# Image pooling on 96 partitions, two channel products instead of six, sink values in PSUM, and the order of two queues

## The chip, the cores and the metric

The kernel runs on one core of one Trainium2 chip. The metric is the device time of one execution in microseconds. Three executions of the kernel before took 2934.99, 2945.84 and 2946.96 us, so the median is 2945.84 us. Engines go by the names of the profile: PE is TensorE's matmul, PEld its weight load, DVE VectorE, ACT ScalarE, POOL GpSimd, SP SyncE, whose queue only issues DMAs.

## What is computed

For 64 batches, an image of 12 channels by 224 by 224 is summed over patches of 16 by 16 and its channels are mixed into 192 features. That gives 14 x 14 = 196 tokens, to which 32 text tokens are appended. Then come a layer norm, causal attention with 12 heads, rotary angles and a sink value per head, a residual, a second norm and a mixture of 8 experts with two choices per token.

```
pooled = x.reshape(B, C, n, 16, n, 16).sum(axis=(3, 5))          # n = 14
h = einsum('bcij,ce->bije', pooled, channel_weights)             # 196 x 192 per batch
h = concat([h, txt], axis=1)                                     # 228 tokens
att = softmax(concat([sink_h, mask(q k^T / 4)]))[..., 1:]        # per head
h = h + (att v W_proj + b_proj) * rezero
h = h + moe(layernorm(h))                                        # top 2 of 8, capacity 4560
```

## The kernel before, in words

There are two passes. Pass 1 takes the batches, pass 2 the experts' rows in 160 tiles. The change touches pass 1 and the setup ahead of it.

Pass 1 is a software pipeline. In step i, batch i is pooled (`p`), batch i-1 is normed, projected to q, k and v, and rotated (`a`), batch i-2 has the maxima of its scores taken (`m`), batch i-3 gets its softmax and attention (`t`), and batch i-4 its output projection, residual, second norm and routing (`z`). Each engine runs a list written out by hand in one order per step: `step_tensor`, `step_scalar`, `step_vector`, `pass1_gpsimd` and `pass1_sync`. Engines meet at semaphores only, and each runs strictly in its own order, so a waiting instruction holds up all that stands behind it.

The image lies on 112 partitions: 3 groups (g) of 4 channels by 28 half patch rows, each partition with 8 image rows of 224 columns. `load_image` (L404) is one DMA of contiguous runs of 8 x 224 numbers, 7168 bytes. On POOL, `fold_image` (L682) adds the lower 4 rows to the upper 4, one instruction of 896 elements a partition for each g. On DVE, `pool_image` (L497) sums what is left to 14 patch columns. On POOL, `spread_patches` (L689) multiplies by the 0/1 table `patch`, which puts each half row's sum into the column of its own patch row; three instructions. On PE, `sum_channels` (L837) then needs 2 x 3 products, for two halves of the tokens and three groups, which also sum the partitions.

The order around it, in each step:

- PE: the scores and `score_t` products, `attend` 0 to 2, `T0 T1 T2` (`turn_qk`, L894), `turn_shift` (L934), `make_v`, `turn_y`, `T3 T4 T5`, `sum_channels`, `turn_yn` (L998), and from the next step on `S0 C0`, `project` and so on.
- DVE: `norm1_stats`, `max_scores` 0, `residual`, `norm2_stats`, maxima 1 and 2, `pool_image` 0, `rotate` 0, maximum 3, `pool_image` 1, `rotate` 1, maxima 4 and 5, `choose`, maximum 6, `pool_image` 2, maxima 7 and 8, `make_shift` (L573), `assign` (L659), `place_k` 1, `split_shift` (L583), `weigh` (L638), `place_k` 3, `normalize` 0 and 1 (L589), `place_k` 5.
- ACT, late in the step: `place_q` 0, `copy_y`, `round_shift`, `place_q` 2, `copy_v`, `place_q` 4, `copy_h`, `copy_yn`.
- POOL: `inverse_std` of norm 1, fold 0, `inverse_std` of norm 2, fold 1, `add_rotation` 0, fold 2, `add_rotation` 1, `low_parts` 0 and 1 (L722), `spread_patches`, and four indirect DMAs of `scatter_rows`.
- SP: `load_image` of the batch after `p`, `store_h2`, `load_text` of `p`, and in the first 20 steps `fill_slots`, which writes 1453.5 KB of filler rows to HBM.

Waits that matter here: `turn_shift` waits for `shift_made` and for `routed`, which `assign` raises with its fifth instruction (L675). `turn_yn` waits for `y_normed` of `normalize` 1. `split_shift` waits for `shift_rounded` of ACT. `T0` waits for `qk_low` of both `low_parts`. `choose` uses and `weigh` writes small operands in columns 32 to 63 of PSUM bank 7.

Of the kernel before, what the change touches and what calls it, by code (L numbers as in the profile page):

```python
# [21 lines left out]
GRP = 4  # L22
NG = CH // GRP
XP = GRP * SIDE * 2
XF = HALF * IMG
D = 192
# [22 lines left out]
def constants(tokens):  # L49
# [29 lines left out]
    rows = np.arange(XP)  # L79
# [10 lines left out]
        "patch": ((rows[:, None] // 2) % SIDE == np.arange(SIDE)[None]).astype(f),  # L90
# [5 lines left out]
               "before", "patch", "filler"]  # L96
# [28 lines left out]
def build(nc, x, txt, chan_w, norm_scale, norm_bias, w_attn, b_attn, w_proj, b_proj, sinks,  # L125
# [17 lines left out]
    with ctx:  # L143
# [23 lines left out]
        patch = sb("patch", [XP, SIDE])  # L167
        filler = sb("filler", [TT, 2, 2, RW], u32)
        chan = sb("chan", [XP, NG, D])
# [5 lines left out]
        sink_tok = sb("sink_tok", [TT, HEADS])  # L175
        sink_key = sb("sink_key", [128, HEADS])
# [5 lines left out]

        arena = sb("arena", [128, 2 * NG * XF])
        xin = [arena[0:XP, NG * XF * i:NG * XF * (i + 1)].rearrange("p (g f) -> p g f", g=NG) for i in range(2)]
        pooled = [sb(f"pooled{i}", [XP, NG, SIDE]) for i in range(2)]
        spread = sb("spread", [XP, NG, SIDE * SIDE])
# [68 lines left out]
        def view(parts, a, b):  # L255
            nonlocal taken
            taken += a * b
            assert taken <= 2 * NG * XF
            return arena[0:parts, taken - a * b:taken].rearrange("p (a b) -> p a b", a=a)
# [41 lines left out]
        x_spread = sem("x_spread")  # L301
# [52 lines left out]
        N_SMALL = 25  # L354


        def setup_sync(sp):
            for dst, src in (
                (cos[:, :, :], const["cos"]), (sin[:, :, :], const["sin"]), (ident[:, :], const["ident"]),
                (split[:, :], const["split"]), (small[:, :], const["small"]),  # L360
                (patch[:, :], const["patch"]), (filler[:, :, :, :], const["filler"]),
# [38 lines left out]
        x_img = x.rearrange("b (g c) (q r) w -> b (c q) g (r w)", g=NG, r=HALF)  # L400
# [23 lines left out]
        def setup_vector(dve):  # L424
# [28 lines left out]
            nc.vector.tensor_scalar(sink_tok[:, :], sink_tok[:, :], 4.0, None, ALU.mult)  # L453
# [43 lines left out]
        def pool_image(dve, at, g):  # L497

            if g == 0:
                wait(dve, x_spread, at.b - 1)  # L500
# [1202 lines left out]
```

## Time and profile before

| | |
|---|---|
| three executions | 2934.99, 2945.84, 2946.96 us |
| the profiled execution: time | 2942.38 us |
| its span, first to last instruction | 2940.6 us |
| busy share PE, DVE, POOL, ACT | 95%, 70%, 69%, 58% |
| mean granted TensorE clock | 0.983 of full speed |
| pass 1, from the first channel product to the last `turn_shift` | 42.0 to 1724.8 us |

A row of the timeline is the start in us, the duration in us, the engine, the line, the operation, output<-input, the shapes and xcount, which is the number of instructions merged into the row; in brackets stands the idle time before it and what ended it. The end of a PE row is modelled and overlaps the next row, so intervals on PE are read from start to start. A PE product on plain fp32 data appears as two records. A DMA row of a window gives the packets, the MB and the share of sixteen DMA engines' time that the queue's packets took.

### The profile page before, as it was taken

The page shows a single profiled execution, that of the slowest core. Times are in us where ns is not written, and L with a number is a line of the kernel's source. Part 1 is how long each engine was busy: PE and PEld are TensorE (multiplying, and loading weights), DVE is VectorE, ACT ScalarE, POOL GpSimd, SP SyncE. Part 2 cuts the span into 40 slices and gives each one's busy share as a digit, 9 for nine tenths or more (in the row PEclk, how much of TensorE's full clock was granted, in tenths as well). Part 3 has the DMA queues.
Part 4 walks back from the last instruction along what each step waited for, and adds up shares of the span by engine and source line. Part 5 has one row for each costly group of instructions (what it writes and reads, how often), then busy time and mean ns, then how long its engine had stood idle before and what let it go on. Part 6 is the DMA issues. An engine that isn't in the chain of part 4 may idle for free. (4 is left out here: it accounts for less than half of the span.)

```text
span 2940.6 us, 65980 instructions
## 1 busy us (share of the span) xinstructions
PE 2788.6 (95%) x21712; PEld 2515.0 (86%) x21712; DVE 2049.6 (70%) x5657; ACT 1692.5 (58%) x4074; POOL 2022.5 (69%) x2070
## 2 busy tenths in 40 slices
PE   2899999999999999999999976999999999999998
PEld 1788888888888888888888866999999989999997
DVE  3577777777777777777777745767676767676766
ACT  1466666666665666666566644655565656565655
POOL 3578888888888888788888733655566555565655
PEclk9899999999999999999999988999999999999999
DMA  6455455544443444444344222333333333323242
GB/s 191 141 176 175 167 165 173 156 122 122 115 107 106 119 121 122 119 111 111 107 121 121 56 48 61 56 60 51 63 55 65 49 65 49 65 45 65 46 68 43
DMA packets 206006, 292.47 MB, mean 99 GB/s; under 512 B 95670, under 2 KB 167675, under 8 KB 205874
## 3 DMA queue, kind: packets, MB, share of 16 engines
q1 hardware_dynamic: 82642, 241.41, 28.2%
q0 software_dynamic: 122880, 47.00, 11.4%
q10 hardware_dynamic: 352, 2.41, 0.3%
q8 instruction: 69, 1.13, 0.2%
q14 instruction: 63, 0.52, 0.1%
HBM read 201.73 MB, written 93.90 MB: 101 GB/s over the span
## 5 line engine op out<-in xcount | busy, mean ns | idle before, releaser
L1493 POOL DMA_INDIRECT out<-arena,who x320 | 595.3, 1860 | 291.4 <-DVE who L1372 180.5
L571 DVE TENSOR_REDUCE top<-bank 114x2 f32<-114x456 f32 (+1 forms) x576 | 352.8, 622 | 87.3 <-PE bank L930 71.1
L686 POOL TENSOR_TENSOR arena<-arena 112x896 f32<-112x896 f32 x192 | 403.0, 2100 | 13.2 <-DMA arena<-in_x 13.2
L1466 PE MATMUL bank<-w_dn,hid 128*114 128x192 f32 x3840 | 401.9, 264 | 0.0
L1466 PEld LDWEIGHTS bank<-w_dn,hid 128*114 128x114 f32 x3840 | 390.3, 180 | 0.0
L1439 ACT ACTIVATE arena<-bank 128x456 f32<-128x456 f32 x320 | 176.3, 551 | 342.1 <-PE bank L1430 332.2
L1284 POOL DMA_INDIRECT moe_rows<-row,slot x256 | 294.4, 1150 | 103.9 <-issue 85.0
L548 ACT ACTIVATE pieces<-bank 64x456 fp32r<-64x456 f32 x384 | 209.4, 545 | 147.1 <-PE bank L906 144.9
L1443 DVE TENSOR_TENSOR arena<-bank,arena 128x456 f32<-128x456 f32 x320 | 201.5, 630 | 96.6 <-ACT arena L1439 84.6
L726 POOL TENSOR_TENSOR qk<-rot_c,qk 114x384 fp32r<-114x384 f32 x256 | 253.8, 1013 | 19.0 <-ACT qk L747 19.0
L1426 PE MATMUL bank<-pieces 128*128 128x456 f32 x640 | 241.2, 377 | 21.9 <-DVE arena L1443 15.2
L805 ACT ACTIVATE prob<-bank 115x456 f32<-115x456 f32 x384 | 208.0, 542 | 78.0 <-PE bank L956 77.3
L1430 PE MATMUL bank<-pieces 128*128 128x456 f32 x640 | 238.5, 373 | 0.0
L1455 DVE TENSOR_TENSOR hid<-arena,hid 128x456 fp32r<-128x456 f32 x320 | 201.6, 630 | 52.3 <-ACT hid L1450 34.3
L1429 PE MATMUL bank<-pieces 128*128 128x456 f32 x640 | 237.9, 372 | 0.0
L1450 ACT ACTIVATE hid<-arena 128x456 fp32r<-128x456 f32 x320 | 186.9, 584 | 88.1 <-DVE arena L1443 86.7
L1428 PE MATMUL bank<-pieces 128*128 128x456 f32 x640 | 237.5, 371 | 0.0
L1427 PE MATMUL bank<-pieces 128*128 128x456 f32 x640 | 236.8, 370 | 0.0
L1483 POOL TENSOR_TENSOR rms<-rms,minus_half 114x4 f32<-114x4 f32 x82 | 85.4, 1042 | 193.5 <-DVE rms L1364 193.5
L906 PE MATMUL bank<-ident_r,qk 114*128 114x114 f32 x1536 | 202.1, 282 | 10.7 <-POOL qk L726 10.7
L502 DVE TENSOR_REDUCE pooled<-arena 112x14 f32<-112x896 f32 x192 | 206.5, 1076 | 6.4 <-POOL arena L686 6.4
L906 PEld LDWEIGHTS bank<-ident_r,qk 114*128 114x128 f32 x1536 | 186.5, 196 | 23.0 <-POOL qk L726 23.0
(171 smaller groups left out, 7216.3 us busy)
## 6 DMA issues: line engine op xcount, KB each, us to landing
arena<-in_x SPq DMA_DIRECT2D x63, 2352.0 KB, 11.8
arena<-moe_rows SPq DMA_DIRECT2D x82, 363.4 KB
moe_rows<-filler SPq DMA_DIRECT2D x20, 1453.5 KB
out<-h SPq DMA_DIRECT2D x64, 171.0 KB
out<-arena,who POOLq DMA_INDIRECT x320, 5.0
arena<-in_w_t SPq DMA_DIRECT2D x9, 512.0 KB
arena<-in_w_t SPq DMA_DIRECT2D x18, 256.0 KB
moe_rows<-row,slot POOLq DMA_INDIRECT x256, 7.3
```

The costliest lines, as they stand in the source:

```text
L571: nc.vector.tensor_reduce(dst, src, AX.X, ALU.max).then_inc(maxed[k], 1)
L686: nc.gpsimd.tensor_tensor(xin[at.par][:, g, 0:mid], xin[at.par][:, g, 0:mid], xin[at.par][:, g, mid:XF], ALU.add).then_inc(x_folded, 1)
L726: ins = nc.gpsimd.tensor_tensor(lo, of, first.bitcast(fp32), ALU.subtract)
L906: ins = nc.tensor.matmul(dst[:, TT * (2 * pair + half):TT * (2 * pair + half + 1)], src, ident_r[0:TT, 0:TT], start=True, stop=True)
L1284: nc.gpsimd.indirect_dma_start(out=moe_rows[0:SLOTS, :], out_offset=bass.IndirectOffsetOnAxis(ap=slot[at.par][:, 2 * t + k:2 * t + k + 1], ...
L1426: nc.tensor.matmul(dst, hi[:, 0, col], za_hi[:, :], start=True, stop=False)
L1427: nc.tensor.matmul(dst, hi[:, 0, col], za_lo[:, :], start=False, stop=False)
L1428: nc.tensor.matmul(dst, lo[:, 0, col], za_hi[:, :], start=False, stop=False)
L1429: nc.tensor.matmul(dst, hi[:, 1, col], zb[:, :], start=False, stop=False)
L1430: ins = nc.tensor.matmul(dst, lo[:, 1, col], zb[:, :], start=False, stop=True)
L1466: ins = nc.tensor.matmul(dst, hid2[:, j, h_part, at], w_dn2[e_par][:, j, w_part, :], start=(j == 0 and s % 2 == 0 and part == 0), stop=(j ...
L1493: nc.gpsimd.indirect_dma_start(out=out[:, :], out_offset=bass.IndirectOffsetOnAxis(ap=who[par][:, s:s + 1], axis=0), in_=ys[par][:, s, :], ...
```

## The change

- The image lies on 96 partitions instead of 112: partition 12 r + c holds channel c, the two image rows 2r and 2r+1 of each of the 14 patch rows. `load_image` is 8 DMAs, one for each r, each to 12 partitions in runs of 1792 bytes (`x_loaded` counts 8 x 16).
- `fold_image` and `pool_image` work in bands of patch rows, 5, 5 and 4 of 14. A fold has 1120, 1120 and 896 elements a partition; `pool_image` reduces over 16 neighbouring columns alone.
- `spread_patches`, the table `patch` and the semaphore `x_spread` are gone. `sum_channels` has 2 products with 96 rows to sum over; `chan` holds each channel's weights 8 times over and is loaded by one DMA.
- `sink_tok` times 4 is written to columns 480 to 491 of PSUM bank 7, and `make_shift` reads it there.
- DVE: `assign` moves from behind `make_shift` to ahead of maxima 7 and 8, where `pool_image` 2 was; `pool_image` 2 moves behind `place_k` 1, ahead of `split_shift`.
- POOL: fold 2 moves from between the two `add_rotation` to behind `low_parts` 1, where `spread_patches` was.

```diff
-GRP = 4
-NG = CH // GRP
-XP = GRP * SIDE * 2
-XF = HALF * IMG
+XP = CH * HALF
+XF = 2 * IMG
+BANDS = ((0, 5), (5, 10), (10, SIDE))
+NG = len(BANDS)
...
+        sink_top = bank[7][0:TT, 480:480 + HEADS]
...
-            for g in range(NG):
-                sp.dma_start(chan[:, g, :], chan_w[GRP * g:GRP * (g + 1), :].unsqueeze(1)
-                             .to_broadcast([GRP, SIDE * 2, D])).then_inc(loaded, 16)
+            sp.dma_start(chan[:, :], chan_w.unsqueeze(0).to_broadcast([HALF, CH, D])).then_inc(loaded, 16)
...
-        x_img = x.rearrange("b (g c) (q r) w -> b (c q) g (r w)", g=NG, r=HALF)
+        x_img = x.rearrange("b c (i r s) w -> b r c i (s w)", r=HALF, s=2)
...
             wait(sp, x_pooled, NG * (at.b - 1))
-            sp.dma_start(xin[at.par][:, :, :], x_img[at.b, :, :, :]).then_inc(x_loaded[at.par], 16)
+            for r in range(HALF):
+                sp.dma_start(xin[at.par][CH * r:CH * (r + 1), :, :], x_img[at.b, r, :, :, :]).then_inc(x_loaded[at.par], 16)
...
-            nc.vector.tensor_scalar(sink_tok[:, :], sink_tok[:, :], 4.0, None, ALU.mult)
+            nc.vector.tensor_scalar(sink_top, sink_tok[:, :], 4.0, None, ALU.mult)
...
             ins = nc.vector.tensor_reduce(
-                pooled[at.par][:, g, :],
-                xin[at.par][:, g, 0:XF // 2].rearrange("p (r j c) -> p j r c", r=HALF // 2, c=PATCH), AX.XY, ALU.add)
+                pooled[at.par][:, SIDE * lo:SIDE * hi],
+                xin[at.par][:, lo:hi, 0:IMG].rearrange("p i (j c) -> p i j c", c=PATCH), AX.X, ALU.add)
...
-                                    sink_tok[:, :].unsqueeze(1).unsqueeze(1).to_broadcast([TT, 2, 2, HEADS]),
+                                    sink_top.unsqueeze(1).unsqueeze(1).to_broadcast([TT, 2, 2, HEADS]),
...
-            mid = XF // 2
-            nc.gpsimd.tensor_tensor(xin[at.par][:, g, 0:mid], xin[at.par][:, g, 0:mid], xin[at.par][:, g, mid:XF],
+            lo, hi = BANDS[g]
+            nc.gpsimd.tensor_tensor(xin[at.par][:, lo:hi, 0:IMG], xin[at.par][:, lo:hi, 0:IMG], xin[at.par][:, lo:hi, IMG:XF],
                                     ALU.add).then_inc(x_folded, 1)
...
-            pe.wait_ge(x_spread, n)
+            pe.wait_ge(x_pooled, NG * n)
             wait(pe, v_ready, at.b)
             for t, (lo, hi) in enumerate(((0, TT), (TT, SIDE * SIDE))):
-                for g in range(NG):
-                    ins = nc.tensor.matmul(bank[6][0:hi - lo, D * t:D * (t + 1)], spread[:, g, lo:hi], chan[:, g, :],
-                                           start=(g == 0), stop=(g == NG - 1))
+                ins = nc.tensor.matmul(bank[6][0:hi - lo, D * t:D * (t + 1)], pooled[at.par][:, lo:hi], chan[:, :],
+                                       start=True, stop=True)
...
             maxima("6")
-            if p:
-                pool_image(dve, p, 2)
+            if z:
+                assign(dve, z)
             maxima("7 8")
             if m:
                 make_shift(dve, m)
-            if z:
-                assign(dve, z)
             if a:
                 place_k(dve, a, 1)
+            if p:
+                pool_image(dve, p, 2)
             if m:
                 split_shift(dve, m)
...
                 if a:
                     add_rotation(pool, a, 0)
-                if p:
-                    fold_image(pool, p, 2)
-                if a:
                     add_rotation(pool, a, 1)
                     low_parts(pool, a, 0)
                     low_parts(pool, a, 1)
                 if p:
-                    spread_patches(pool, p)
+                    fold_image(pool, p, 2)
```

## Rows read from the trace of the kernel before

**Rows 1.** The page's part 1: busy us, share of the span, instructions.

```profile
PE 2788.6 (95%) x21712; PEld 2515.0 (86%) x21712; DVE 2049.6 (70%) x5657; ACT 1692.5 (58%) x4074; POOL 2022.5 (69%) x2070
```

**Rows 2.** Busy time of a stretch of pass 1 by engine, clock, DMA share, GB/s.

```profile
700.00:1200.00 500.00, 494.62 (x4240) 436.86 (x4243) 372.02 (x1127) 304.99 (x678) 404.63 (x504) 1.00 0.43 117
```

**Rows 3.** Timeline of PE, from one step's T0 into the next step.

```profile
1005.77 1.55 PE L906 MATMUL bank<-ident_r,qk 114*128 114x114 f32 x12
...
1010.74 2.16 PE L844 MATMUL bank<-chan,spread 112*114 112x192 f32 x12
1012.74 0.56 PE L1003 MATMUL bank<-ident,yn 114*97 114x114 f32 x4
...
1031.33 1.55 PE L906 MATMUL bank<-ident_r,qk 114*128 114x114 f32 x12
1033.21 0.39 PE L939 MATMUL bank<-ident,shift 114*128 114x114 f32 x2 [0.33 <-DVE slot L675]
```

**Rows 4.** PE timeline: the channel products of two steps, 57 steps apart.

```profile
211.91 2.16 PE L844 MATMUL bank<-chan,spread 112*114 112x192 f32 x12
...
1680.88 2.16 PE L844 MATMUL bank<-chan,spread 112*114 112x192 f32 x12
```

**Rows 5.** Idle time of PE before L939, 195:1740: ended by, us, times.

```profile
  DVE slot L675: 12.5, 35
```

**Rows 6.** Timeline of DVE at make_shift in the same two steps.

```profile
1005.98 0.21 DVE L578 TENSOR_TENSOR shift<-top,sink_tok 114x48 f32<-114x48 f32 x1
...
1031.51 0.60 DVE L578 TENSOR_TENSOR shift<-top,sink_tok 114x48 f32<-114x48 f32 x1
```

**Rows 7.** Timeline of POOL: low_parts 1, spreads, a fold, spreads of the next step.

```profile
1003.58 1.99 POOL L726 TENSOR_TENSOR qk<-rot_c,qk 114x384 fp32r<-114x384 f32 x2 [0.27 <-ACT qk L747]
1005.52 1.53 POOL L694 TENSOR_TENSOR spread<-pooled,patch 112x196 f32<-112x196 f32 x3
...
1023.66 2.11 POOL L686 TENSOR_TENSOR arena<-arena 112x896 f32<-112x896 f32 x1
...
1031.05 1.48 POOL L694 TENSOR_TENSOR spread<-pooled,patch 112x196 f32<-112x196 f32 x3
```

**Rows 8.** PE timeline of the first step that has no image.

```profile
1701.44 1.55 PE L906 MATMUL bank<-ident_r,qk 114*128 114x114 f32 x12
...
1707.79 0.63 PE L1003 MATMUL bank<-ident,yn 114*97 114x114 f32 x4 [1.30 <-DVE yn L598]
```

**Rows 9.** DVE timeline of that step, from split_shift on.

```profile
1704.34 0.45 DVE L586 SCALAR_TENSOR_TENSOR shift_t<-shift_hi,split,bank 128x228 fp32r<-128x228 f32 x1 [1.01 <-ACT shift_hi L795]
...
1707.31 0.42 DVE L598 TENSOR_TENSOR yn<-bank,rden 114x96 f32<-114x96 f32 x2
```

**Rows 10.** Instructions of L502 (pool_image): durations ns min/median/max.

```profile
L502 DVE TENSOR_REDUCE pooled<-arena x69: 1073/1077/1078, 709.1 to 1287.7; 112x14 f32<-112x896 f32 x69
```

**Rows 11.** Hardware queue in 305.5:309.5 (fillers), 1006:1016 (one image), 1752:1760 (weights), 300:500.

```profile
q1 hardware_dynamic: 321, 0.52, 37.3%
...
q1 hardware_dynamic: 352, 2.41, 88.0%
...
q1 hardware_dynamic: 1069, 1.44, 84.2%
...
q1 hardware_dynamic: 12159, 32.08, 47.4%
```

**Rows 12.** Windows of a filler step: DMA share and GB/s are the last two columns.

```profile
306.00:309.00 3.00, 3.00 (x38) 2.59 (x37) 2.40 (x12) 2.18 (x6) 2.27 (x3) 1.00 0.38 135
...
305.00:306.00 1.00, 1.00 (x10) 0.92 (x9) 0.35 (x1) 0.04 (x1) 1.00 (x3) 1.00 0.24 69
325.00:326.00 1.00, 1.00 (x7) 0.60 (x4) 0.02 (x1) 0.73 (x2) 1.00 (x2) 1.00 0.15 48
```

**Rows 13.** Start of the run: first channel products on PE, first norm statistics on DVE.

```profile
42.00 4.16 PE L844 MATMUL bank<-chan,spread 112*114 112x192 f32 x12 [7.65 <-DMA w_qkv<-rot_s]
...
50.36 0.62 DVE L515 BATCH_NORM_STATS2 st<-h 114x6 f32<-114x192 f32 x2 [10.87 <-DMA h<-in_txt]
```

More of the change, by code:

```diff
@@ L78, in constants @@
             filler[:, par, s, COL_ID] = tokens + (par * T + 2 * q + s) % ROWS
-    rows = np.arange(XP)
     return {
@@ L89, in constants @@
         "before": (q[:, None] < q[None, :]).astype(f),
-        "patch": ((rows[:, None] // 2) % SIDE == np.arange(SIDE)[None]).astype(f),
         "filler": filler,
@@ L95 @@
 CONST_NAMES = ["cos", "sin", "ident", "mask_q0", "mask_k", "sel", "split", "small",
-               "before", "patch", "filler"]
+               "before", "filler"]
 class Batch:
@@ L166, in build @@
         ones = sb("ones", [TT, TT], bf16)
-        patch = sb("patch", [XP, SIDE])
         filler = sb("filler", [TT, 2, 2, RW], u32)
-        chan = sb("chan", [XP, NG, D])
+        chan = sb("chan", [XP, D])
         scale_col = sb("scale_col", [C, 2])
@@ L179, in build @@
         gate = sb("gate", [C, 2, E])
[L183 to L186, printed above, removed]
+        arena = sb("arena", [128, 2 * SIDE * XF])
+        xin = [arena[0:XP, SIDE * XF * i:SIDE * XF * (i + 1)].rearrange("p (i f) -> p i f", i=SIDE) for i in range(2)]
+        pooled = [sb(f"pooled{i}", [XP, SIDE * SIDE]) for i in range(2)]
         h = [sb(f"h{i}", [TT, 2, D]) for i in range(2)]
@@ L257, in view @@
             taken += a * b
-            assert taken <= 2 * NG * XF
+            assert taken <= 2 * SIDE * XF
             return arena[0:parts, taken - a * b:taken].rearrange("p (a b) -> p a b", a=a)
@@ L300, in build @@
         x_pooled = sem("x_pooled")
-        x_spread = sem("x_spread")
         h_summed = sem("h_summed")
@@ L352, in build @@
         added = [sem(f"added{i}") for i in range(2)]
-        N_SMALL = 25
+        N_SMALL = 22
         def setup_sync(sp):
@@ L360, in setup_sync @@
                 (split[:, :], const["split"]), (small[:, :], const["small"]),
-                (patch[:, :], const["patch"]), (filler[:, :, :, :], const["filler"]),
+                (filler[:, :, :, :], const["filler"]),
                 (scale_col[:, :], norm_scale.rearrange("(c p) -> p c", p=C)),
@@ L499, in pool_image @@
             if g == 0:
-                wait(dve, x_spread, at.b - 1)
+                wait(dve, h_summed, at.b - 1)
             dve.wait_ge(x_folded, NG * at.b + g + 1)
+            lo, hi = BANDS[g]
             ins = nc.vector.tensor_reduce(
-                pooled[at.par][:, g, :],
-                xin[at.par][:, g, 0:XF // 2].rearrange("p (r j c) -> p j r c", r=HALF // 2, c=PATCH), AX.XY, ALU.add)
+                pooled[at.par][:, SIDE * lo:SIDE * hi],
+                xin[at.par][:, lo:hi, 0:IMG].rearrange("p i (j c) -> p i j c", c=PATCH), AX.X, ALU.add)
             ins.then_inc(x_pooled, 1)
@@ L682, in fold_image @@
         def fold_image(pool, at, g):
-            pool.wait_ge(x_loaded[at.par], 16 * (at.half + 1))
-            mid = XF // 2
-            nc.gpsimd.tensor_tensor(xin[at.par][:, g, 0:mid], xin[at.par][:, g, 0:mid], xin[at.par][:, g, mid:XF],
+            pool.wait_ge(x_loaded[at.par], 16 * HALF * (at.half + 1))
+            lo, hi = BANDS[g]
+            nc.gpsimd.tensor_tensor(xin[at.par][:, lo:hi, 0:IMG], xin[at.par][:, lo:hi, 0:IMG], xin[at.par][:, lo:hi, IMG:XF],
                                     ALU.add).then_inc(x_folded, 1)
-        def spread_patches(pool, at):
-            wait(pool, h_summed, at.b)
-            for g in range(NG):
-                pool.wait_ge(x_pooled, NG * at.b + g + 1)
-                ins = nc.gpsimd.tensor_tensor(spread[:, g, :].rearrange("p (i j) -> p i j", j=SIDE),
-                                              pooled[at.par][:, g, :].unsqueeze(1).to_broadcast([XP, SIDE, SIDE]),
-                                              patch[:, :].unsqueeze(2).to_broadcast([XP, SIDE, SIDE]), ALU.mult)
-            ins.then_inc(x_spread, 1)
         def inverse_std(pool, at, norm):
```

1 line of the change is left out of this document (removed).

## The prediction

> **What bounds the kernel now.** I read the page's busy shares first, then the busy time of a stretch of pass 1, then the timelines of PE, DVE and POOL in one step, and last the DMA queues. PE is busy 95% of the span [rows 1] and 98.9% of 500 us in the middle of pass 1, at full clock [rows 2]; no other engine passes 81% there. So PE's own list sets the step. The PE timeline shows how strictly: from one T0 (L906 at 1005.77) to the next at 1031.33 are 25.56 us, and the one idle time of a step is a wait of 0.33 us at `turn_shift` for `assign`'s L675, present in one step and absent in the other [rows 3]. Starts of L844 at 211.91 and 1680.88 are 57 steps apart, so the mean step is 25.77 us [rows 4]. The wait stands in 35 steps of the 60 from 195 us on, 12.5 us in all [rows 5]. It comes where `make_shift` took 0.60 us instead of 0.21 [rows 6]. In the long case it was issued at 1031.51, inside the three spreads that began at 1031.05 on POOL [rows 7].
>
> On the length of `make_shift` the Trainium skill (SBUF — State Buffer, Who interferes with whom) says that a VectorE instruction with two SBUF inputs waits for the whole of a GpSimd instruction that reads SBUF. The trace agrees: 0.39 us more, less than one spread of some 0.5 us. By that rule a `make_shift` that still read two SBUF tiles beside fold 2, 2.11 us long, could stand still for up to 2 us; with the sink values in PSUM it shouldn't.
>
> **PE's part.** `sum_channels` takes 12 records, from 1010.74 to 1012.74, 2.00 us for six products [rows 3]. Two products stay: 0.67 us. PE's list gets 1.33 us shorter. The wait at `turn_shift` goes too, since `assign` is done before maxima 7 and 8: its six instructions take about as long as the `pool_image` 2 that stood there, 1.08 us [rows 10], so `make_shift` stays at its time. PE alone would then need 25.56 - 1.33 = 24.2 us.
>
> **What is late next: `turn_yn`.** In the first step without an image PE finds nothing between T5 and `turn_yn`, and there it idles 1.30 us for DVE's `normalize` 1: T0 at 1701.44, `turn_yn` at 1707.79, 6.35 us [rows 8]. DVE runs there without a gap from `split_shift` at 1704.34 to L598 at 1707.31 [rows 9], and `split_shift` hangs on ACT's `round_shift`, which hangs on T0. The change shortens nothing of that. In a step with an image `turn_yn` now comes 12.74 - 5.77 = 6.97 us after T0 [rows 3]. After: 0.67 us of products put PE there at 6.97 - 1.33 = 5.64, and it waits until 6.35. So of 1.33 us only about 0.6 arrive, plus the removed wait.
>
> **Moved: fold 2 and `pool_image` 2.** POOL ends `low_parts` 1 at about 1005.52, 0.25 us ahead of T0 [rows 3, 7]. Fold 2 keeps 896 elements, 2.11 us [rows 7], and ends 1.85 us after T0. `pool_image` 2 waits for it behind `place_k` 1 (done 1.75 after T0, since T1 lands at about 1.2) and holds DVE 1.0 us, until 2.9. `split_shift` was issued 1704.34 - 1701.44 = 2.90 after T0 [rows 8, 9]. The two come out even; I add 0.03. Behind `pool_image` 2 stand `split_shift`, `weigh`, `place_k` 3 and `normalize`, and PE waits for these, so each 0.1 us of a later fold 2 is 0.1 us a step. Bounds for fold 2 on rows of 224: at the rate of the contiguous fold, 2.11; at the dearest strided rate on POOL, 1.0 us for 384 elements (half of 1.99) [rows 7], 2.3. I take 2.11 and keep 0.2 for the range. The four scatters start at 2.1 instead of 1.4 after T0 and end at 7.5; `inverse_std` of norm 1 isn't wanted before 7.95. SP gets its release for the next image 4 us later, against a step of slack.
>
> **The longer folds 0 and 1.** 1120 elements cost 2.11 x 1.25 = 2.6 us on POOL, 0.5 more each, and about 1.3 us on DVE, 0.24 more each [rows 7, 10]. On POOL fold 2 (2.1) goes from the middle and the spreads (1.5) from the end. The norm chain starts 0.5 us earlier relative to `turn_yn`, which pays for the first fold, and `add_rotation` 0 finds POOL free just when its input comes. `low_parts` 1 hangs on ACT as before [rows 7], so T0 doesn't move. I cost it at nothing; if that cover is gone, it is 0 to 0.3 us a step. The PSUM operand of `make_shift`: between -0.4 and +0.1 us on DVE, none of it on the path.
>
> **The sum of a step.** From `turn_yn` to the next T0, 1031.33 - 1012.74 = 18.59 us [rows 3], PE without a gap, plus 0.06 that the products behind a stall lose. T0 to `turn_yn` 6.35 + 0.03. That is 25.0 us against 25.77, and 61 steps have both an image and a `normalize`: 0.77 x 61 = 47 us.
>
> **DMAs in the first 20 steps.** One image moves as 352 packets in 88.0% of 16 engines' 10 us: 141 us of engine time, 0.40 us a packet, on all 16 engines [rows 11]. Fillers from 114 partitions keep the share at 0.38, six of sixteen engines [rows 12], at 74 ns a packet [rows 11], so the number of engines follows the partitions. Six is the largest divisor of 114 up to 16; by that, an image DMA of 12 partitions uses 12. These six engines carry all: 918 filler packets are 68 us or 11.4 each; residual rows, 171 KB in shorter runs, some 10 us or 1.6 each; the image 7.4 beside fillers (1.0 x 47.4% x 25.8 us x 16 = 196 us of a step, less 68 and 10, over 16) [rows 11]. With the scatters they are busy from about 305.1 to 325.5, 20.4 of 25.8 us [rows 12]. After, the image is 1344 packets of 1792 bytes. Fixed cost and rate from two mixes (352 packets with 2.41 MB in 141 us; 1069 with 1.44 MB in 108 us) [rows 11] are 28 ns and 0.054 ns a byte, 125 ns a packet; without fixed cost, and at the quicker pace beside fillers, 84 ns. So 9.4 to 14 us on each of 12 engines, and 22.4 to 27.0 a step where 25.0 are to be had. I take 112 ns, 12.5 us, 25.5 us in all: nearly even. The loss is 20 x 0.5 less some 4 us of slack, about 5 us. Later steps have no fillers and half the time is free (8.8 us of engine time, then up to 14).
>
> On this the Trainium skill (DMA: Bandwidth & Descriptors, Why a DMA increments its semaphore by 16 and not by 1) says that a queue uses the largest number up to 16 that divides the slowest dimension of both sides. Its outcome is the 12 above, so it speaks against the change; the share of 0.38 agrees for 114 partitions, no row shows it for 12. Were it wrong and all 16 used, the loss of 5 us would be nothing.
>
> **Start.** The first products take 4.16 us in twelve records [rows 13]; a third stays, -2.8, and -1.3 in each of the next two steps. The first norm waits 10.87 us for a text that stands behind an image in the queue [rows 13]; that image takes up to 6 us longer, I take +4. Three setup DMAs fewer: 0 to -2. Together -2.
>
> **The forecast.** 2942.4 - 47 + 5 - 2 = 2898 us against the profiled execution, which is 3.5 us under the median of 2945.84; against that it is 1.6% less. Own range 2884 to 2916: start 6, fold 2 up to 0.2 x 61 = 12, DMA 0 to 15.
>
> **Rivals.**
> 1. DMA-bound filler steps. Each 0.1 us that the six engines need beyond 25.0 costs 2 us in all. At 27.0 it is 36 us: 2930. Slower than before only if a packet takes over 135 ns: 13.0 + 15.1 = 28.1 us a step, 20 x 3.1 - 4 = 58 us. Scattered rows could do that: at 150 ns, 29.8 us a step, 92 us lost, 2985. For: runs a quarter as long. Against: filler packets of 1632 bytes take 74 ns, though they are written. Chance 0.19.
> 2. `pool_image` 2 comes later than reckoned (fold 2 slower, or begun later): 0.3 us a step, 18 us, 2916; at 0.8 us the gain is gone. Chance 0.08.
> 3. PE's full saving: DVE isn't what `turn_yn` waits for. Step 24.2, 96 us less, 2850. The idle time of [rows 8] speaks against it. Chance 0.03.
> 4. No effect, because some other chain holds the step near 25.7: 2940. Between T0 and the next T0 PE is idle 0.33 us and no more [rows 3]. Chance 0.05.
>
> **Chances.** Forecast 0.65. A difference under 0.5%, 15 us, can hardly be told from none here. Faster: 0.65 + 0.09 + 0.07 + 0.03 + 0.01 = 0.85. Within: 0.04 + 0.01 + 0.03 = 0.08. Slower: 0.06 + 0.01 = 0.07. The range for 8 in 10 is 2878 to 2936, which takes in the mild half of rival 1.
>
> **What would show it.** L844: 4 records a step; `turn_shift` without a wait; `turn_yn` with 0.7 us of idle time ended by L598; L502's last band ending at `split_shift`; steps of 25.0 us. Image landing some 4 us later, and a DMA share that stays at 0.75 while only images move. Wrong if the first 20 steps are longer than the later ones by over 0.5 us, if `split_shift` waits for L502 over 0.1 us, or if idle time moves to T0.

## The result, and the profile after

The changed kernel takes 3498.21 us (median of 4 runs, 3478.84 to 3507.85) where the kernel before takes 2944.28: 1.188 times as long, 95% interval 1.184 to 1.193. The forecast was 2898 us, 1.6% less, with a range that ended at 2936. The time lies some 560 us outside it, on the other side.

The page of the kernel after, with the parts that answer to [rows 1], and the stretch that answers to [rows 2] (columns as there: stretch, length, busy time of PE, PEld, DVE, ACT and POOL, granted clock, DMA share, GB/s):

```profile
span 3489.1 us, 65814 instructions
...
PE 2931.0 (84%) x21200; PEld 2584.0 (74%) x21200; DVE 2081.9 (60%) x5657; ACT 1702.7 (49%) x4074; POOL 1983.1 (57%) x1878
...
DMA  6677767777776666666667666214333333333333
```

```profile
700.00:1200.00 500.00, 397.37 (x3026) 336.39 (x3026) 282.70 (x829) 228.63 (x504) 294.19 (x334) 0.86 0.70 101
```

PE's busy share in pass 1 fell from 98.9% to 79%, its granted clock from 1.00 to 0.86, and the DMA share rose from 0.43 to 0.70, while the transfer rate fell from 117 to 101 GB/s. More time of the DMA engines for fewer bytes a second: that is the first thing to see, and it points at the transfers themselves.

What PE waited for, by groups of its instructions (busy us and mean ns, then the idle time in front of them and what ended it), and the waits of PE for the maxima, of DVE for texts and of ACT for scatters (us in total, times, longest):

```profile
L1006 PE MATMUL bank<-ident,row 114*96 114x114 f32 x256 | 50.4, 337 | 130.8 <-ACT row L756 130.8
...
L988 PE MATMUL bank<-ident,yn 114*97 114x114 f32 x256 | 42.9, 293 | 57.8 <-DVE yn L594 57.8
```

```profile
DVE st L511 <- DMA h<-in_txt: 261.2, 27, 27.7
...
PE bank L904 <- DVE top L567: 185.0, 20, 12.9
...
ACT row L756 <- DMA moe_rows<-row,slot: 171.8, 32, 7.1
```

The extra 548 us of the span (3489.1 against 2940.6) can be booked on PE. Its idle time grew by 548 - (2931.0 - 2788.6) = 406 us. Its busy time grew by 142 us although the channel products shrank from 144 to 57 us; so some 229 us are other instructions that ran longer, at a mean granted clock of 0.903 against 0.983. Of the idle time 185 us stand in 20 waits for the maxima on DVE, 131 us in waits for ACT's `row`, and 58 us at `turn_yn` (5.0 before).

The two large ones are waits for DMAs, one engine removed. First `row`. Timeline of all engines in one step after the fillers, cut to five lines:

```profile
1208.88 1.55 PE L891 MATMUL bank<-ident_r,qk 114*128 114x114 f32 x12
...
1210.90 1.19 POOL L1266 DMA_INDIRECT moe_rows<-row,slot  x1 [0.21 <-issue]
...
1211.98 7.58 SPq L401 DMA_DIRECT2D arena<-in_x  x8
...
1228.83 0.98 ACT L756 ACTIVATE row<-h,shifted,rstd 114x192 f32<-114x192 f32 x2 [4.39 <-DMA moe_rows<-row,slot]
...
1229.87 0.97 PE L1006 MATMUL bank<-ident,row 114*96 114x114 f32 x4 [2.95 <-ACT row L756]
```

The buffer of `row` may only be written again when the scatters that read it have landed. They were issued from 1210.90 on, together with the image, and landed only at 1228.8. Behind its wait of 2.95 us PE runs slowly: the four records of L847 take 2.77 us, where in the part of the step ahead of the wait they took 1.55. The granted clock of the next four microseconds is 0.58, so for most of them it was the lower of its two levels, 1.2 GHz, and then 2.4 GHz again:

```profile
1226.00:1230.00 4.00, 1.05 (x9) 0.83 (x8) 2.78 (x4) 1.17 (x3) 1.56 (x3) 0.99 0.78 114
1230.00:1234.00 4.00, 4.00 (x14) 2.67 (x15) 0.55 (x2) 2.04 (x5) 0.00 (x0) 0.58 0.80 102
1234.00:1238.00 4.00, 4.00 (x47) 3.54 (x46) 2.73 (x13) 1.99 (x6) 3.08 (x4) 1.00 0.79 95
```

Second, the maxima, in a step with fillers (the same view):

```profile
453.28 10.88 SPq L406 DMA_DIRECT2D h<-in_txt  x1
...
478.13 0.62 DVE L511 BATCH_NORM_STATS2 st<-h 114x6 f32<-114x192 f32 x2 [11.09 <-DMA h<-in_txt]
...
479.81 0.70 PE L904 MATMUL bank<-mask_q,ident_r 114*114 114x456 f32 x1 [8.27 <-DVE top L567]
```

The text's DMA instruction stood at SP for 10.88 us, behind image and fillers in a full queue. DVE's norm statistics wait 11.09 us for that text, the maxima stand behind them on DVE, and PE waits 8.27 us for a maximum.

Both come from one number: how long an image takes. In 22 us in which the hardware queue moves the image and little else, a text of 24 KB (packets, MB, share of 16 engines):

```profile
q1 hardware_dynamic: 1276, 2.10, 74.9%
```

12 of 16 engines are busy all the time, as forecast. Over all packets of the queue this is 0.749 x 22 x 16 / 1276 = 207 ns each. But the queue also carries packets of 4 bytes, about one to every 14 of the image's, which take some 27 ns here, so this mean is too low for the image. Taken from the trace by size, the packets of 1792 bytes alone take 223 ns, in this window and over all steps behind the fillers; 112 were forecast. The rate is 95 GB/s, and an image of 2.41 MB takes 25 us, as long as a whole step, where it took 10 before [rows 11].

Steps, from one start of the channel products to the next: 39.84 us on average over the first 20 (26.53 before), 32.03 us after (25.77 before).

### The profile page after: what moved, and what is told of

The parts are those of the page before. It is cut to its first block and busy times, and to the rows that moved or that the text cites. A ratio compares the mean times of both kernels' runs of the same rounds, so it can differ in the third digit from the quotient of the medians.

```text
span 3489.1 us, 65814 instructions
## 1 busy us (share of the span) xinstructions
PE 2931.0 (84%) x21200; PEld 2584.0 (74%) x21200; DVE 2081.9 (60%) x5657; ACT 1702.7 (49%) x4074; POOL 1983.1 (57%) x1878
## 3 DMA queue, kind: packets, MB, share of 16 engines
q10 hardware_dynamic: 1440, 2.41, 0.5%
## 5 line engine op out<-in xcount | busy, mean ns | idle before, releaser
L682 POOL TENSOR_TENSOR arena<-arena 96x1120 f32<-96x1120 f32 (+1 forms) x192 | 462.1, 2408 | 40.1 <-DMA arena<-in_x 40.1
L705 POOL TENSOR_TENSOR rot_c<-rot_c,rot_s 114x192 f32<-114x192 f32 x256 | 145.2, 588 | 337.1 <-DVE rot_s L531 337.1
L691 POOL TENSOR_TENSOR var<-mv,ln_eps 114x2 f32<-114x2 f32 x128 | 25.1, 196 | 429.0 <-DVE mv L515 429.0
L1408 PE MATMUL bank<-pieces 128*128 128x456 f32 x640 | 240.1, 375 | 22.0 <-DVE arena L1425 14.2
L498 DVE TENSOR_REDUCE pooled<-arena 96x70 f32<-96x1120 f32 (+1 forms) x192 | 236.3, 1232 | 36.3 <-POOL arena L682 32.6
L847 PE MATMUL bank<-w_qkv,xn_t 97*114 97x384 f32 x512 | 254.6, 631 | 3.5 <-DVE rot_s L531 2.2
L511 DVE BATCH_NORM_STATS2 st<-h 114x6 f32<-114x192 f32 x256 | 79.1, 351 | 295.8 <-DMA h<-in_txt 261.2
L529 DVE TENSOR_TENSOR rot_c<-bank,cos 114x384 f32<-114x384 f32 x128 | 71.4, 558 | 293.8 <-PE bank L847 293.8
L904 PE MATMUL bank<-mask_q,ident_r 114*114 114x456 f32 x192 | 84.8, 442 | 185.0 <-DVE top L567 185.0
L748 ACT ACTIVATE xn<-h,shifted,rstd 114x192 f32<-114x192 f32 x128 | 63.1, 541 | 357.4 <-POOL shifted L697 357.4
L1412 PE MATMUL bank<-pieces 128*128 128x456 f32 x640 | 237.4, 371 | 0.0
L1411 PE MATMUL bank<-pieces 128*128 128x456 f32 x640 | 237.2, 371 | 0.0
```

The costliest lines, as they stand in the source:

```text
L498: ins = nc.vector.tensor_reduce(pooled[at.par][:, SIDE * lo:SIDE * hi], xin[at.par][:, lo:hi, 0:IMG].rearrange("p i (j c) -> p i j c", c=P ...
L682: nc.gpsimd.tensor_tensor(xin[at.par][:, lo:hi, 0:IMG], xin[at.par][:, lo:hi, 0:IMG], xin[at.par][:, lo:hi, IMG:XF], ALU.add).then_inc(x_f ...
L847: ins = nc.tensor.matmul(bank[6][0:TT, 0:2 * D], xn_t[:, c, TT * t:TT * (t + 1)], w_qkv[:, c, 0:2 * D], start=(c == 0), stop=(c == 1))
L1408: nc.tensor.matmul(dst, hi[:, 0, col], za_hi[:, :], start=True, stop=False)
L1411: nc.tensor.matmul(dst, hi[:, 1, col], zb[:, :], start=False, stop=False)
L1412: ins = nc.tensor.matmul(dst, lo[:, 1, col], zb[:, :], start=False, stop=True)
```

## The experiments

Four questions were open: why a packet is slow, what the moved order costs, what the number of DMAs costs, and whether the small parts do what they should. The kernel before ran beside each group, at 2942.55 to 2954.54 us. With one run of a kernel its time is given alone.

### The image DMA: one or eight, long runs or short, neighbours or spread

**One DMA, long runs**, the rest as in the changed kernel:

```diff
-            for r in range(HALF):
-                sp.dma_start(xin[at.par][CH * r:CH * (r + 1), :, :], x_img[at.b, r, :, :, :])...
+            sp.dma_start(xin[at.par].rearrange("p i f -> p (i f)"), x_img[at.b, :, :])...
```

> The changed kernel, but each image comes in one DMA to all 96 partitions, 25,088 neighbouring bytes a partition, so the pooled numbers are sums of other pixels; volume, shapes and all other work are unchanged. Theory: the whole loss (3498 against 2944 us) is the image DMA, which takes some 25 us where 12 were forecast, and the working of the step on the engines holds. Then the step is 25.0 us, turn_yn idles 0.7 us for L594, and the time is 2893 us (2880 to 2906). Rival: the fold and pool order itself holds the step; then it stays above 2944 us with a quick image DMA.

Measured: 3082.35 us, ratio 1.044 (1.039 to 1.050). The image is fast again, 13.3 us from issue to landing, but the expected 2893 didn't come; the time is what the rival foretold, above 2944 with a quick image. ACT's `row` still waits for the scatters, 142.2 us in 50 waits (18.7 in 15 before). The hardware queue in the ten microseconds beside the scatters:

```profile
q1 hardware_dynamic: 89, 2.21, 96.1%
```

That is 0.961 x 160 / 89 = 1.73 us a packet. The scatters share the engines with packets that hold one for 1.7 us each, and `row` starts 17.2 us after T0 in the median step instead of 14.5. So some 415 us of the loss go with the image's DMA. Whether the rest is the order or the long packets, this run alone can't tell; the one with short runs below does.

**Eight DMAs, long runs**, twelve neighbouring partitions each:

```diff
             for r in range(HALF):
-                sp.dma_start(xin[at.par][CH * r:CH * (r + 1), :, :], x_img[at.b, r, :, :, :])...
+                sp.dma_start(xin[at.par][CH * r:CH * (r + 1), :, :].rearrange("p i f -> p (i f)"),
+                             x_img[at.b, CH * r:CH * (r + 1), :])...
```

> As e1, but in eight DMAs to 12 neighbouring partitions each, still 25,088 neighbouring bytes a partition; the pooled numbers are again sums of other pixels. Three theories on the 207 ns that a packet of 1792 bytes took. Place: twelve neighbouring partitions share few ways into SBUF; then the image still takes about 25 us and the time is 3300 to 3500. Run: short runs in HBM are slow; then the image takes 12 us or less and the time is about 2895. Engines: only 12 of 16 take part and eight DMAs are issued; then a third more than one DMA's 9 us, 12 us, and 2895 to 2910.

Measured: 3911.73 us, image some 27 us; Place has the image right and the time too low (3300 to 3500). Long runs don't help: with the partitions of the change, the image is as slow as in the changed kernel, and with the long packets the waits for the scatters are the worst seen (580.7 us in 33). The length of the runs is not what makes the image slow.

**One DMA, short runs.** The 96 partitions are written at once, in 14 runs each, again from other pixels:

```diff
+        x_img = x.rearrange("b c h w -> b (c h w)").rearrange("b (g p f) -> b p g f", p=XP, f=XF)
...
+            sp.dma_start(xin[at.par][:, :, :], x_img[at.b, :, :, :]).then_inc(x_loaded[at.par], 16)
```

> As e1, one DMA to 96 partitions, but in 14 runs of 1792 bytes a partition, 172,032 bytes apart, so 1344 packets as in the changed kernel; the pooled numbers are sums of other pixels. Place: packets cost 105 to 125 ns on 16 engines, the image 9 to 11 us, the time 2890 to 2910. Run: packets cost about 207 ns, the image 17 us, filler steps some 31 us, the time about 3010 or more. Engines: as Place.

Measured: 2930.98 us; steps of 26.11 us in the first 20 and 25.66 after; an image lands in 14.0 us. Of the hardware queue in ten of them:

```profile
q1 hardware_dynamic: 1180, 2.11, 89.7%
```

0.897 x 160 / 1180 = 122 ns a packet (all 1180 are of 1792 bytes), 211 GB/s, with the very runs of 1792 bytes of the change. That clears the short runs. The packet is what Place expected, the time is 21 us above its 2890 to 2910. Against the run with one DMA and long packets it is 151 us less, so those are the price of the long packets. `row` still waits a little for the scatters, 59.1 us in 53 waits, at most 1.8.

**Eight DMAs, partitions spread.** Each DMA writes twelve partitions that lie 8 apart; the channel weights are laid out to match, so the right pixels are pooled, as in the changed kernel:

```diff
-                sp.dma_start(xin[at.par][CH * r:CH * (r + 1), :, :], x_img[at.b, r, :, :, :])...
+                sp.dma_start(xin[at.par][r:XP:HALF, :, :], x_img[at.b, r, :, :, :])...
-            sp.dma_start(chan[:, :], chan_w.unsqueeze(0).to_broadcast([HALF, CH, D]))...
+            sp.dma_start(chan[:, :], chan_w.unsqueeze(1).to_broadcast([CH, HALF, D]))...
```

> The changed kernel with the same eight DMAs of 12 partitions and runs of 1792 bytes, but partition 8c + r in place of 12r + c, so that the twelve of one DMA stand 8 apart; chan is repeated to match, and the output is the reference's. Place: the twelve reach about twice to three times as many ways into SBUF; packets 110 to 130 ns, the image 13 to 15 us, the time 2895 to 2950. Run, or Engines: nothing changes, about 3490.

Measured: 3127.78 us, ratio 1.059 (1.057 to 1.061). Same bytes, same reads from HBM by each DMA, same packets, same number of DMAs and engines as the change: 370 us less, from the place of the partitions in SBUF alone. The image moves at some 148 GB/s in about 16 us, a little slower than Place allowed (13 to 15), and the time is far above its 2895 to 2950: something else costs too.

**The kernel before with neighbours, and with spread partitions.** To see the place away from the change, the image of the kernel before was cut into 8 DMAs of 14 partitions, once neighbours, once 8 apart:

```diff
-            sp.dma_start(xin[at.par][:, :, :], x_img[at.b, :, :, :]).then_inc(x_loaded[at.par], 16)
+            for r in range(HALF):
+                sp.dma_start(xin[at.par][14 * r:14 * (r + 1), :, :], x_img[at.b, 14 * r:14 * (r + 1), :, :])...
```

> The kernel before, but its image comes as 8 DMAs of 14 neighbouring partitions each instead of one of 112; same bytes, same runs of 7168 bytes. 14 engines a DMA. Theory A (twelve or fourteen neighbouring partitions are slow by their place): image at 90 to 130 GB/s, 19 to 26 us instead of 10, steps above 29 us, total above 3200. Rival B (only the number of engines and the run length count): 14 of 16 engines and long runs, image in some 11.5 us plus 8 issues on SP, total within 1% of 2944.

> The kernel before with its image in 8 DMAs of 14 partitions that lie 8 apart; bytes, runs of 7168 bytes, number of DMAs and of partitions as in e8, so only the place of the partitions differs. Theory A (neighbouring partitions share few ports, and this is the whole of e8's loss): image in 11 to 14 us, total 2944 to 3020. Rival B (eight DMAs, their issues and their rows are what costs): near e8's 3653.

The second has `r:XP:HALF` in both places of the last line. Measured: 3652.6 us with neighbours, 3215.71 us spread. The hardware queue in 16 us of the first and in 9 us of the second:

```profile
q1 hardware_dynamic: 304, 1.60, 80.4%
```

```profile
q1 hardware_dynamic: 295, 1.61, 77.7%
```

100 GB/s against 179, and over all packets of the queue 677 ns against 379. Every fourth of these packets is one of 4 bytes; those of 7168 bytes alone take 910 and 492 ns in the two windows. Before, with one DMA of 112 partitions, they took 419 in the window of [rows 11]. Between the two kernels lie 437 us. Here each DMA also reads other addresses of HBM when its partitions change, so this pair alone would not clear HBM; the pair above does, whose reads are the same.

The second half of the theory, that place is the whole loss, fell: 3215.71 is 270 us above before, though the image lands in some 14 us. So 2943 to 3653 us is two steps: eight DMAs instead of one, and neighbours instead of spread. What the spread version has and the kernel before hasn't is waits whose releaser the profile doesn't see:

```profile
DVE pieces L560 <- remote: 195.5, 59, 4.0
...
ACT pieces L549 <- remote: 167.3, 56, 4.3
...
ACT val L790 <- remote: 50.1, 19, 2.9
```

The same sort stands in the spread version of the change, 133.1 us in 42 waits on ACT's `h`, and is gone in the next group. Over 1 us in all it occurs in three of the kernels run, each with eight image DMAs (75.8 us with the eight long ones), but not in all that have eight. The trace's semaphore events tell one thing more: all these waits are for semaphores that PE's products raise. In the spread version of the change the channel products' semaphore rises 3.2 us (median) after the end of their last record; in the kernel before, and in the changed one, 13 to 14 ns after it. With one DMA and the new order it is 0.6 us. Why it rises late stays open, and so does what eight DMAs cost by themselves.

All in one table, by size from the traces, in the steps behind the fillers: the mean time of the image's own packets, and the time from an image's first packet to its last (median):

| image DMA | bytes of a packet | ns | image, us |
|---|---|---|---|
| 8 x 12 neighbours (the change) | 1792 | 223 | 26.3 |
| 8 x 12, 8 apart | 1792 | 135 | 16.5 |
| 1 x 96 | 1792 | 124 | 12.1 |
| 8 x 14 neighbours | 7168 | 864 | 23.3 |
| 8 x 14, 8 apart | 7168 | 505 | 14.2 |
| 1 x 112 (before) | 7168 | 425 | 9.9 |
| 8 x 12 neighbours | 25,088 | 3022 | 27.0 |
| 1 x 96 | 25,088 | 1731 | 11.6 |

What the pairs show is that a DMA on neighbouring partitions moves at 95 to 100 GB/s and one on spread partitions at 150 to 210, whatever its runs. The Trainium skill (SBUF — State Buffer, Door 1: The DMA port swizzle) offers a reason: SBUF has 16 ports for DMAs, four neighbouring partitions share one, and a port carries 32 bytes at 850 MHz. By that, as an estimate from the page, twelve neighbours reach three ports and 82 GB/s, fourteen reach four and 109, and partitions 8 apart reach eight and 218. The runs agree in order, not closely in size: 95, 100, and 156 to 179. The 95 is more than three ports would carry by the page, and there the measurement decides. No trace here shows the ports; that the place of the partitions is the cause is shown, that it works through ports is not.

### The order: fold 2, pool_image 2 and assign at their old places

```diff
             maxima("6")
-            if z:
-                assign(dve, z)
+            if p:
+                pool_image(dve, p, 2)
             maxima("7 8")
             ...
+            if z:
+                assign(dve, z)
             if a:
                 place_k(dve, a, 1)
-            if p:
-                pool_image(dve, p, 2)
```

and on POOL fold 2 back between the two `add_rotation`.

**With the one fast DMA:**

> As e3 (one DMA for the image, 96 partitions, 14 runs of 1792 bytes each, wrong pixels), but fold 2, pool_image 2 and assign stand where they stood before. The image is released some 4 us earlier again. Theory A (the image that lands beside the scatters is what holds norm2_apply): waits of ACT L755 for moe_rows fall from 59 us to under 25, steps reach 25.0 us unless turn_shift waits for assign again (up to 0.3 us), total 2893 to 2915. Rival B (the place in the order costs nothing): steps stay at 25.6 us, total 2930. Rival C (assign behind pool_image 2 now comes too late, make_shift not beside spreads): turn_shift waits 0.3 us in every step, steps 25.3.

Measured: 2898.03 us, ratio 0.984 (0.981 to 0.987), steps of 25.69 and 25.12 us. The waits of `row` for the scatters are gone, not only fewer, and `turn_shift` waits in one step in all. So the new order costs 33 us by these two times, 24 by the two ratios (0.992 and 0.984), since the kernel before ran 12 us faster beside this one; in the profiles the last channel products come 31.5 us later with it. With the sink values in PSUM there was nothing left for it to gain. The waits of `turn_yn` in the new order and in the old one:

```profile
PE bank L987 <- DVE yn L593: 57.7, 63, 2.4
```

```profile
PE bank L987 <- DVE yn L593: 37.6, 64, 2.7
```

That is 0.33 us a step. DVE in the changed kernel, with the scatter on POOL beside it, then DVE in the version with spread fillers below, which has the old order (start, us):

```profile
1211.79 0.45 DVE L582 SCALAR_TENSOR_TENSOR shift_t<-shift_hi,split,bank 128x228 fp32r<-128x228 f32 x1
...
1212.39 1.12 POOL L1266 DMA_INDIRECT moe_rows<-row,slot  x1 [0.30 <-issue]
...
1213.09 0.41 DVE L650 CAST row<-token 114x2 uint32<-114x2 f32 x1
```

```profile
1415.53 0.16 DVE L651 CAST row<-token 114x2 uint32<-114x2 f32 x1
```

`split_shift` is not late: 2.91 us after T0. Behind it a CAST of 114x2 values takes 0.41 us instead of 0.16. It now begins inside a scatter instruction on POOL and ends with it, at 1213.50, where the scatter ends at 1213.51. In the changed kernel 46 of its 64 casts are stretched, and each of them ends 1 to 12 ns before the scatter that it began in; over the run the median is 421 ns against 158. In the old order the scatters begin with T0 instead of 2.0 us after it, no cast begins inside one, and none is stretched. The 0.26 us of the cast are nearly all of the 0.27 us by which `turn_yn` comes later after T0 (6.62 against 6.35, medians of steps with one image DMA).

The waits of ACT's `row` for the scatters are of little weight here: of the 59.1 us, PE's idle time before the product on `row` shows 0.4. What is left of the 31.5 us is mostly PE's own instructions, which are 8 us longer in all.

**With the change's eight DMAs of neighbours:**

> The changed kernel with fold 2, pool_image 2 and assign back at their old places; image in 8 DMAs of 12 neighbouring partitions. Theory A (place of the partitions is the first cause, the later release a second one that adds to it): an image still needs some 25 us of transfer, which is as long as the step, and the release comes 4 us earlier: steps after 20 fall from 32 to 26 to 28, those with fillers stay above 33; total 3050 to 3300. Rival B (release and order count as much as the place): below 3000. Rival C (the order counts for nothing beside the slow transfer): within 1% of 3498.

Measured: 3397.79 us. 100 us less than the change, steps of 30.5 us after the fillers. None of the three ranges holds: B, that order counts as much as place, falls widest; A's 3050 to 3300 is missed by 98 us, and the 2.9% gained are more than C's 1%. With an image that takes a step's length the old order repairs little.

**With eight DMAs of spread partitions:**

> As e4 (8 DMAs of 12 partitions that lie 8 apart, right pixels), with fold 2, pool_image 2 and assign at their old places, so that the image is released some 4 us earlier. Theory A (release time and scatters matter): the late texts (L511) and the remote waits of copy_h go, steps after 20 fall from 29.3 to 25.5 to 27, total 2930 to 3020. Rival B (the eight issues on SP and twelve engines hold it whatever the release): within 1% of e4's 3128.

Measured: 2947.64 us, ratio 1.002 (1.001 to 1.004). Steps after the fillers 25.14 us, the remote waits gone; those with fillers 28.16. A packet beside the scatters:

```profile
q1 hardware_dynamic: 925, 1.56, 68.3%
```

That is 118 ns over all packets; those of 1792 bytes alone take 125 ns here and 132 over the steps behind the fillers, where 112 were forecast and 125 was the upper bound.

### The steps with fillers

The 28.16 us are late texts again: 12 waits of L511, 54.3 us. SP stands for some 20 us in the eight image issues of such a step, 7.6 in others. The fillers come from 114 partitions and use six engines [rows 12]. So they were cut into 112 and 2:

```diff
-            sp.dma_start(rows_e[at.b, :, :, :], filler[:, at.par, :, :]...
+            for lo, hi in ((0, 112), (112, TT)):
+                sp.dma_start(rows_e[at.b, lo:hi, :, :], filler[lo:hi, at.par, :, :]...
```

> As e9 (8 image DMAs of 12 partitions 8 apart, old order, sinks in PSUM, two products), and each filler DMA of 114 partitions is split into one of 112 and one of 2. Theory A (steps with fillers are long, 28.2 us against 25.1, because six engines carry the fillers while texts and images stand behind them in the queue): the filler DMA uses 16 engines, steps with fillers fall to 25.3 to 26.5, total 2890 to 2915. Rival B (it is the number of bytes or the length of the queue behind SP, not the number of engines): steps with fillers 27.5 or more, total 2935 or more.

Measured: 2905.96 us, ratio 0.987 (0.985 to 0.989). From the fourth step on, steps with fillers take 25.1 us like all others, and the eight image issues on SP take 7.6 us there. Three microseconds of fillers, where six engines gave a share of 0.38 and 135 GB/s before [rows 12]:

```profile
452.00:455.00 3.00, 3.00 (x38) 2.55 (x37) 1.82 (x11) 1.60 (x5) 2.94 (x4) 1.00 0.72 225
```

This version pools the right pixels and is faster than both kernels. Its stretch of pass 1:

```profile
700.00:1200.00 500.00, 488.37 (x4208) 422.72 (x4208) 383.01 (x1158) 317.75 (x700) 406.31 (x460) 1.00 0.53 119
```

Cutting the stores of `h2` in the same way as well:

```diff
-            sp.dma_start(out_b[at.b, :, :, :], h2[at.par][:, :, :])...
+            for lo, hi in ((0, 112), (112, TT)):
+                sp.dma_start(out_b[at.b, lo:hi, :, :], h2[at.par][lo:hi, :, :])...
```

> As e10, and the stores of h2 (114 partitions) are split into 112 and 2 in the same way. Theory A: the text of a step stands behind the store, so it lands a little earlier in filler steps: 0 to 10 us less than e10. Rival B: two more issues a step on SP, each 0.8 us, push the image later: equal to e10 or up to 10 us more.

Measured: 2902.88 us, ratio 0.986 (0.984 to 0.989). Not told apart from the version without it.

### The sink values in PSUM, alone

```diff
-            nc.vector.tensor_scalar(sink_tok[:, :], sink_tok[:, :], 4.0, None, ALU.mult)
+            nc.vector.tensor_scalar(sink_top, sink_tok[:, :], 4.0, None, ALU.mult)
...
-                                    sink_tok[:, :].unsqueeze(1).unsqueeze(1)...
+                                    sink_top.unsqueeze(1).unsqueeze(1)...
```

> The kernel before with one part of the change: the scaled sink values are written to spare PSUM columns and make_shift reads them there. Image, products and order as before. Theory A (make_shift is stretched only when both its inputs lie in SBUF beside a GpSimd instruction): it takes 0.2 us in every step, assign ends 0.37 us earlier, the idle time of PE before L939 goes: 35 x 0.36 = 12.5 us less, ratio 0.996. Rival B (the stretch has nothing to do with sink_tok): make_shift still 0.6 us in every other step, ratio 1.000.

Measured: 2925.94 us, ratio 0.994 (0.992 to 0.996), so theory A. `make_shift` in this kernel and in the kernel before (ns, least, median, most):

```profile
L579 DVE TENSOR_TENSOR shift<-top,bank x64: 203/204/206, 96.3 to 1707.4; 114x48 f32<-114x48 f32 x64
```

```profile
L578 DVE TENSOR_TENSOR shift<-top,sink_tok x64: 207/588/614, 98.6 to 1723.4; 114x48 f32<-114x48 f32 x64
```

PE's idle time before `turn_shift` falls from 12.5 us in 35 steps [rows 5] to 1.4 us in one, the last step, where the kernel before has it too. So 11.1 us of waiting are gone; by the medians the kernel is 16.6 us faster. One line gives two fifths of what the best version gives (0.6% of 1.4).

## Why the prediction was wrong

- **DMAs in the first 20 steps: this step failed, and with it the forecast.** The count of engines was right: 12 of 16, share 0.75. The term that was mis-sized is the packet of 1792 bytes: 84 to 125 ns, taken as 112, measured 223 (207 with the 4-byte packets of the queue in the mean). The bounds came from an image on 112 partitions at once and from fillers on 114; no row of before shows a DMA that reaches only a few neighbours. The prediction asked how many engines a DMA gets and not which partitions it reaches. The counts of [rows 11] also hold 4-byte packets (352 is 336 of the image and 16 of these), and the lower bound of 84 should be 88 by its own 196 less 68 and 10.
- **On spread partitions the 112 would not quite have held either:** 132 to 135 ns. The prediction's own sum at 132 gives 14.8 + 13.0 = 27.8 us a filler step, 20 x 2.8 - 4 = 52 us lost, and 2945 in all, no gain. Measured with the old order are 28.16 us a filler step and 2947.64 in all: close to that sum, though the waits seen in those steps are late texts. Fillers cut into 112 and 2 bring 2906.
- **"Later steps have half the time free": false**, by the same mis-sized packet. At 25 us an image fills the step with or without fillers, and the loss there, 6.3 us in each of 43 steps, is half of all. The prediction let transfers cost only where their sum fills the step. But two things in a step have a due time of their own: the scatters, which `row` waits for (131 us of PE's idle time), and the text, which the norm and behind it the maxima wait for (185 us). Both stand beside or behind the image.
- **Rival 1** named the mechanism, a packet over 135 ns, and its price at 150 ns, 2985 us. Its own formula at 223 ns (223 x 1344 / 12 = 25.0 us beside 13.0 us of fillers and rows: 38.0 a step) gives 20 x 13.0 - 4 = 256 us for the filler steps; 39.84 us a step were measured, not far from 38.0. The size of the packet was off, and the rival stopped at the filler steps.
- **Moved, fold 2 and `pool_image` 2: even, as said,** for `split_shift` (2.91 us after T0, 2.90 forecast). What failed is "against a step of slack" for SP's release, and the scatters' later start at no cost: with a fast image the order costs 24 to 33 us. Some 20 of them (0.33 x 61) stand at `turn_yn`, most of it the CAST that begins inside a scatter, which the prediction didn't price.
- **`turn_yn`: right.** It is what is late next: with the old order it comes 6.34 us after T0 (1417.66 - 1411.32), forecast 6.38, in the changed kernel 6.61. PE's full saving (rival 3) never came.
- **PE's part, the longer folds, the sum of a step: right** once the image is fast and the old order is back: steps are 25.12 us against 25.0. In the order that the prediction spoke of, a fast image gives 25.66. Folds 0 and 1 take 2.57 us and fold 2 2.09, and L829 has four records.
- **The wait at `turn_shift`** goes, but by the PSUM operand alone; moving `assign` wasn't needed. The prediction gave the operand no gain on the path, and it has 11.1 of the 12.5 us and 16.6 in the medians. Its reading that the long `make_shift` was issued inside the spreads holds for the short one too, issued at 1005.98 where they run from 1005.52 to 1007.05 [rows 6, 7]. The trace shows two outcomes of one meeting: as a rule the long `make_shift` ends some 65 ns behind the second spread, and in the short cases the second spread itself takes 0.57 us instead of 0.52.
- **Start:** the first channel products come at 60.12 us instead of 42.00, where +4 less 2.8 was forecast; with the fast DMA they come at 39.79.

The total of 2898 us is that of the version with one fast image DMA and the old order, 2898.03, which pools other pixels. In the order of the change the fast image gives 2931. That 2898 comes out so closely is chance: the forecast was for another order, and had 5 us for the DMAs and a start of -2 in it.

What the loss is made of: place of the partitions 370 us with the new order (3498 to 3128) and 450 with the old one (3398 to 2948); order 100 us with neighbours, some 170 to 180 with spread partitions and 24 to 33 with one DMA. Eight spread DMAs instead of one cost 197 us with the new order (2931 to 3128) and 50 with the old one (2898 to 2948), of which 42 go when the fillers are cut into 112 and 2; the versions with one DMA read other pixels, in other strides. Stalls feed each other, so the parts don't add up.

## What to carry to other kernels

Before cutting a transfer by partitions, ask which partitions one DMA reaches, not only how many engines it gets: twelve neighbours moved at 95 GB/s, the same twelve rows 8 partitions apart at some 150. For each transfer write down what has a due time beside it and behind it in the queue; a transfer that doubles its length costs first through those, and the engine clock adds to it. And run the small part of a change alone: one operand in PSUM was worth 0.6% by itself. Last, a mean over all packets of a queue isn't the time of the packet you reckon with: compare MB over packets with the bytes of a run first.

## What the runs showed of the hardware that was not expected

- A transfer's packet of 1792 bytes takes 223 ns when its DMA writes twelve neighbouring partitions and 132 to 135 ns on twelve that lie 8 apart; one of 7168 bytes 864 and 505 ns on fourteen. In the changed kernel a high DMA share (0.70) so stood beside a low rate (101 GB/s).
- Packets of 25 KB (1.73 us each) delay a scatter that shares their engines: `row` starts 17.2 us after T0, 15.2 with packets of 1792 bytes in the same order.
- A DVE CAST of 114x2 values takes 0.16 us by itself; in the changed kernel 46 of the 49 that began inside a scatter instruction on POOL lasted until 1 to 12 ns before its end, 0.42 us.
- A stall of PE of 2.95 us is followed by four microseconds at a granted clock of 0.58. Over the run 229 us of longer instructions stand beside 406 us of added idle time.
- In three kernels with eight image DMAs, consumers wait up to 4.3 us at a time, 413 us in one of them, for semaphores of PE that rise 1.6 to 4.3 us after the end of the products' last record, where 13 to 14 ns are seen in the kernel before. It was not explained.
